# A graph-network kernel whose two planes of edge sums are merged before their product

## The chip, the cores and the metric

One Trainium2 chip, one of its cores. The metric is the device time of one execution in microseconds; lower is better. Five engines work side by side from lists of their own and meet at semaphores: TensorE (PE in the profile; its weight loads are PEld), VectorE (DVE), ScalarE (ACT), GpSimd (POOL) and SyncE (SP, which only issues DMAs here). SBUF is the memory on the chip, with 128 partitions; PSUM holds TensorE's results.

## The reference, cut to what matters

There are 12,500 nodes with 128 features and 200,000 edges, sorted by their target `dst`. Each edge has 64 features for the first layer and 128 for the second.

```python
h = relu(layernorm(x))
aggregated = segment_sum(edge_attr_64 @ W_edge.T, dst) / clip(degree, 1)
x = x + concat([h @ W_self.T, aggregated @ W_neigh.T]) @ W_final.T + b_final
h = relu(layernorm(x))
agg = segment_sum(edge_attr_128, dst)
x = x + relu(concat([h, agg]) @ W1 + b1) @ W2 + b2
```

`degree` is the number of edges that a node receives. All is fp32.

## The kernel before

**Sums over the edges.** The edges are cut into 128 chunks of 12 or 13 units of 128 edges. For every chunk VectorE compares the targets, counted from the first target of a batch, with 0 to 63 (`one_hots`, L1013), which gives a 128 x 64 one-hot matrix a unit. TensorE multiplies each unit's features with it (`sums`, L631, L633, L649): the 128 features of the second layer and the 64 of the first, summed by node into a window of 64 nodes. The degrees come from a product of ones with the sum of the one-hots (L658), which GpSimd adds up (`hot_sums`, L522). VectorE adds each window from PSUM to its place in SBUF (`adds`, L1043), where the first node of the window is only known at run time.

**Three planes.** The sums lie in `agg`, 128 partitions x 3 planes x columns, a column a node. Plane 0 has the 128 features of the second layer. The first layer's sums are spread over planes 1 and 2 so that TensorE's halves can work at once: in plane 1 the features are in partitions 64 to 127 and the degree in 0 to 63, in plane 2 it is the other way round. A node's true sum is the sum of both planes with the halves of one exchanged. `w_c` has a version of the projected weights for each plane, with a column more that picks the degree.

**Groups and ticks.** A tick is one chunk. 25 groups of 512 nodes (the last of `SEQ` has 256) are worked through the two layers as soon as their sums are complete: group q of `SEQ` is taken on tick `TAKE[q]`. Its steps stand at fixed ticks behind that: `neigh` (L694, TensorE, the product of `agg` with `w_c`) at +0, `layer_0` at +1, `stats_2` at +2, `std_2` at +3, `scale_2` at +4, `norm_2` at +5 (L903), its turning by TensorE at +6 (L669) and ScalarE's copy at +7, `hidden` at +8 (L706, L708) and +9 (L918), `output` at +10 (L715), `result` at +11 (L1157) and the store at +12. The part of the layer that needs no edges (`stats_1` to `own_part`, L678, and ScalarE's copies L883 and L890) starts at tick `SELF[q]`, some nine ticks before. On each engine the tick's own work on the chunk (`sums` on TensorE) comes first and these steps behind it, except on VectorE, where the steps come ahead of the tick's `adds`. Nothing is moved at run time: what waits, holds up all that is behind it on its engine.

**What binds ticks to each other.** `sums` use three banks of PSUM in turn, so they wait for the adds of three ticks before. One-hots are made three ticks ahead, edges are loaded into five slots (L394), so that a load waits for the sums five ticks before. `neigh` waits for all adds of the ticks before its own and, in some groups, for a `fold` (L1112, L1114). The columns of a finished group are cleared by GpSimd for another (`CLEARS`). Two groups, 8 and 9 (q = 22 and 23), have two sets of columns (`BOTH`) and twice the products.

Of the kernel before, what the change touches and what calls it, by code (L numbers as in the profile page):

```python
# [14 lines left out]
P = 128  # L15
# [60 lines left out]
def build_gnn(nc, x, dst, edge_attr_128, edge_attr_64, W_self, W_neigh, W_edge, W_final, b_final,  # L76
# [73 lines left out]
    for q, g in enumerate(SEQ):  # L150
        for at, other in ((FIRST_W, g + 4 if g and g in LOWER else 0), (UPPER_AT, g - 4 if g in UPPER else 0)):
            if other in (LOWER if at == FIRST_W else UPPER) and other:
                a = at + (g - 1) % 4 * GW
                CLEARS.append((TAKE[q] + 9, a, a + GW))
# [7 lines left out]
    def bounds(t):  # L162
# [4 lines left out]
        if SIDE[t] == "bottom":  # L167
            lo = min(g for g in free if g) if 1 not in free else 0
            hi = lo
            while hi + 1 in LOWER and hi + 1 in free and (hi < 4 or TAKE[TURN[hi - 3]] + 11 <= t):  # L170
                hi += 1
# [7 lines left out]
        while lo - 1 in UPPER and lo - 1 in free and (lo - 1 > NG - 5 or TAKE[TURN[lo + 3]] + 11 <= t):  # L179
            lo -= 1  # L180
# [41 lines left out]
    for t in range(TICKS):  # L222
        for q in range(NG):
            if t == TAKE[q] + 6:
                tp_use["n", q] = len(tp_use)
            if t == TAKE[q] + 10:
# [24 lines left out]
    with ExitStack() as ctx:  # L251
# [19 lines left out]
        own = sb("own", [P, GN, D])  # L271
        h2 = sb("h2", [P, GN, D])
# [60 lines left out]
        def ps_tab(q):  # L333
# [14 lines left out]
        s_fold, s_nb, s_deg, s_x1, s_bn2, s_mv2, s_std2, s_rstd2, s_nmr2 = (  # L348
            sem(n) for n in ("s_fold", "s_nb", "s_deg", "s_x1", "s_bn2", "s_mv2", "s_std2", "s_rstd2", "s_nmr2"))
# [93 lines left out]
        def _(pool):  # L443
# [58 lines left out]
            def clear(k, a, b):  # L502
                done = [q for q in range(NG) if TAKE[q] + 9 == k]
# [49 lines left out]
            for t in range(TICKS):  # L553
# [4 lines left out]
                for q in range(NG):  # L558
                    if t == TAKE[q] + 6:
# [12 lines left out]
        def _(pe):  # L572
# [108 lines left out]
            def neigh(q):  # L681
                g = SEQ[q]
                pe.wait_ge(s_added, ADDED[min(CH, TAKE[q])])
                for i, (k, _) in enumerate(FOLDS):
                    if k == q:
                        pe.wait_ge(s_fold, 2 * i + 2)
# [4 lines left out]
                parts = [(a, k) for a in columns_of(g) for k in range(2)]  # L691
# [29 lines left out]
            for t in range(TICKS):  # L721
# [10 lines left out]
                for q in range(NG):  # L732
                    if t == TAKE[q] + 8:
                        hidden(q)
                    if t == TAKE[q] + 10:
# [4 lines left out]
                for q in range(NG):  # L740
                    if t == TAKE[q] + 6:
# [4 lines left out]
                for q in range(NG):  # L746
                    if t == TAKE[q]:
# [62 lines left out]
        def _(act):  # L810
# [80 lines left out]

            def std_2(q):
# [27 lines left out]
            for t in range(TICKS + 1):  # L920
# [3 lines left out]
                for q in range(NG):  # L924
                    if t == TAKE[q] + 12:
                        store(q)
                for q in range(NG):
                    if t == TAKE[q] + 7:
                        turned_2(q)
                    if t == TAKE[q] + 9:  # L930
# [6 lines left out]
                for q in range(NG):  # L937
                    if t == TAKE[q] + 3:
# [387 lines left out]
```

## Time and profile before

| | |
|---|---|
| median of 3 runs | 556.91 us (556.08 to 558.59) |
| profiled execution | 556.97 us |
| its span, first to last instruction | 555.1 us |
| TensorE matmuls busy | 503.9 us, 91% |
| VectorE, GpSimd, ScalarE busy | 390.6, 368.4, 151.5 us |
| mean granted TensorE clock | 0.966 of full speed |
| moved by DMA | 169.53 MB, 305 GB/s on average |

The page has the busy time of each engine, the span in slices, the DMA queues, the chain of work that ended last, and the costliest groups of instructions. "Idle before" is the idle time of an engine in front of an instruction, with the instruction that released it; "issue" means that nothing was found that the engine could have waited for. An fp32 product is two records in the trace. Records of TensorE overlap: their mean is longer than the time from one start to the next.

### The profile page before, as it was taken

How to read it: one execution, taken by the hardware profiler on the slowest of the kernel's cores; microseconds unless marked ns; L12 is line 12 of the kernel's file. 1: busy time of each engine (PE TensorE's matmuls, PEld its weight loads, DVE VectorE, ACT ScalarE, POOL GpSimd, SP SyncE). 2: the span in 40 equal slices, each digit the busy share in tenths (PEclk: the TensorE clock that was granted, in tenths of full speed). 3: DMA queues.
4: the chain of work that ended last, by engine and by line, in shares of the span. 5: the costliest groups of instructions: out<-in, count | busy, mean ns of one | idle time of the engine just before them, and what ended most of it. 6: DMA issues, size and time to landing. Idle time of an engine off the chain costs nothing.

```text
span 555.1 us, 25952 instructions
## 1 busy us (share of the span) xinstructions
PE 503.9 (91%) x10989; PEld 450.1 (81%) x10989; DVE 390.6 (70%) x1230; ACT 151.5 (27%) x353; POOL 368.4 (66%) x524
## 2 busy tenths in 40 slices
PE   5568879899989999999999999998999999999993
PEld 4457768789878898888988898888888888988782
DVE  5434698776896768967798688789669877567322
ACT  0011101332233332342234224333323332313101
POOL 2735947667577776785768777885866765845730
PEclk9767899999999999999999999999999999999996
DMA  8924999999999998999999999999999998959910
GB/s 282 388 58 148 380 354 359 374 339 322 312 347 303 341 349 303 367 301 313 341 323 355 333 331 323 369 320 304 325 320 358 329 322 277 382 221 310 378 41 13
DMA packets 113229, 169.53 MB, mean 305 GB/s; under 512 B 5486, under 2 KB 84310, under 8 KB 113111
## 3 DMA queue, kind: packets, MB, share of 16 engines
q1 hardware_dynamic: 85843, 154.42, 79.7%
q10 hardware_dynamic: 27268, 13.43, 8.3%
q8 instruction: 88, 1.44, 1.1%
q14 instruction: 30, 0.25, 0.1%
HBM read 161.43 MB, written 6.40 MB: 302 GB/s over the span
## 4 chain that ended last, share of the span: by engine, by line
PE 81%; issue 6%; DVE 4%; DVEq 1%; ACT 0%; POOL 0%
PE ps L631 28%; PE ps L649 15%; PE ps L694 9%; PE ps L706 5%; PE ps L633 5%; PE ps L678 5%; PE ps L669 4%; PE ps L715 4%; PE ps L708 4%; DVE agg L1043 2%; PE ps L658 1%; DVE x L1157 1%; DVE onehot L1013 1%; DVE bn L1137 0%; DVEq L1043 0%
## 5 line engine op out<-in xcount | busy, mean ns | idle before, releaser
L631 PEld LDWEIGHTS ps<-onehot,ring 128*64 128x64 f32 x3126 | 198.8, 141 | 30.8 <-issue 22.6
L631 PE MATMUL ps<-onehot,ring 128*64 128x64 f32 x3126 | 217.2, 228 | 6.5 <-issue 4.6
L633 PE MATMUL ps<-onehot,ring 128*64 128x64 f32 x3126 | 217.3, 228 | 4.7 <-issue 4.7
L522 POOL TENSOR_TENSOR hot_part<-onehot 128x384 bf16<-128x384 f32 (+2 forms) x128 | 116.7, 912 | 152.3 <-DVE onehot L1013 150.6
L633 PEld LDWEIGHTS ps<-onehot,ring 128*64 128x64 f32 x3126 | 198.8, 141 | 5.4 <-issue 5.4
L1043 DVE TENSOR_TENSOR agg<-ps,agg 128x128 f32 (+1 forms) x319 | 95.0, 298 | 120.1 <-PE ps L658 95.9
L1013 DVE TENSOR_TENSOR onehot<-iota_win,rel 128x384 f32<-128x384 f32 (+3 forms) x192 | 164.5, 857 | 0.2
L649 PE MATMUL ps<-onehot,ring 128*64 128x64 f32 x3126 | 121.9, 226 | 7.2 <-issue 7.1
L649 PEld LDWEIGHTS ps<-onehot,ring 128*64 128x64 f32 x3126 | 109.2, 141 | 7.4 <-issue 7.2
L694 PEld LDWEIGHTS ps<-w_c,agg 128*128 128x128 f32 x424 | 49.8, 191 | 7.3 <-DVE agg L1043 3.7
L694 PE MATMUL ps<-w_c,agg 128*128 128x129 f32 x424 | 52.3, 276 | 3.3 <-issue 2.3
L522 POOL TENSOR_TENSOR hot_sum<-hot_part 128x128 bf16<-128x128 bf16 x96 | 44.7, 466 | 7.5
L875 ACT ACTIVATE hn<-x,nmr,rstd 128x128 f32<-128x128 f32 x98 | 40.4, 483 | 22.5 <-DVE nmr L1104 22.4
L903 ACT ACTIVATE h<-x,nmr,rstd 128x128 f32<-128x128 f32 x98 | 40.4, 484 | 15.5 <-DVE nmr L1149 15.5
L918 ACT ACTIVATE hid<-ps,b_col 128x512 f32<-128x512 f32 (+1 forms) x25 | 17.0, 679 | 93.2 <-PE ps L708 93.2
L500 POOL TENSOR_TENSOR x<-x,b_bc 128x512 f32<-128x512 f32 (+1 forms) x25 | 35.6, 1424 | 10.2 <-ACT h L903 10.2
L522 POOL TENSOR_TENSOR hot_sum<-hot_sum,hot_part 128x128 bf16<-128x128 bf16 x64 | 34.9, 545 | 5.0
L508 POOL MEMSET agg<- 128x1536 f32 (+2 forms) x26 | 35.5, 1366 | 0.0
L487 POOL TENSOR_TENSOR x<-x,b_bc 128x512 f32<-128x512 f32 (+1 forms) x25 | 34.2, 1369 | 0.0
L883 ACT COPY hT<-ps 128x512 f32<-128x512 f32 (+1 forms) x25 | 14.5, 579 | 70.5 <-PE ps L669 70.5
L890 ACT COPY own<-ps 128x512 f32<-128x512 f32 (+1 forms) x25 | 14.5, 579 | 67.3 <-PE ps L678 64.4
L494 POOL TENSOR_TENSOR x<-x,own 128x512 f32<-128x512 f32 (+1 forms) x25 | 31.9, 1275 | 0.0
(118 smaller groups left out, 568.7 us busy)
## 6 DMA issues: line engine op xcount, KB each, us to landing
ring<-in_edge_attr_dram SPq DMA_DIRECT2D x95, 768.0 KB, 5.5
ring<-in_edge_attr_dram SPq DMA_DIRECT2D x96, 384.0 KB, 7.0
ring<-in_edge_attr_dram SPq DMA_DIRECT2D x32, 832.0 KB, 6.2
ring<-in_edge_attr_dram SPq DMA_DIRECT2D x32, 416.0 KB, 7.7
x<-in_x_dram ACTq DMA_DIRECT2D x23, 256.0 KB, 6.3
out_dram<-x ACTq DMA_DIRECT2D x23, 256.0 KB
x<-in_dst_dram SPq DMA_DIRECT2D x1, 384.0 KB
x<-in_dst_dram SPq DMA_DIRECT2D x1, 208.0 KB, 3.6
```

The lines of the kernel that those rows point to most:

```text
L487: nc.gpsimd.tensor_tensor(rows, rows, b0_bc[:, :].unsqueeze(1).to_broadcast([P, nt, D]), ALU.add).then_inc(s_xb, 1)
L500: nc.gpsimd.tensor_tensor(rows, rows, b2_bc[:, :].unsqueeze(1).to_broadcast([P, nt, D]), ALU.add).then_inc(s_x1b, 1)
L508: nc.gpsimd.memset(agg[:, :, a:b], 0.0).then_inc(s_zero, 1)
L522: nc.gpsimd.tensor_tensor(out, a, b, ALU.add).then_inc(s_hotsum, 1)
L631: nc.tensor.matmul(bank[0:H, o:o + WIN], ring128[0:K, slot, u, 0:H], hots, start=u == 0, stop=r == R - 1, skip_group_check=True)
L633: nc.tensor.matmul(bank[H:P, o:o + WIN], ring128[0:K, slot, u, H:D], hots, start=u == 0, stop=r == R - 1, skip_group_check=True)
L649: nc.tensor.matmul(bank[feats, o:o + WIN], ring64[0:K, slot, u, :], onehot[0:K, hot, u, :], start=False, stop=True, skip_group_check=True)
L694: last = nc.tensor.matmul(ps_nb[:, j // 2, j % 2, :], agg[:, 1 + k, a + j * P:a + (j + 1) * P], w_c[:, k, :], start=i == 0, stop=i == len( ...
L875: last = nc.scalar.activation(hn[:, j, :], x0[:, j0 + j, :], ACT.Relu, bias=nmr1[:, u, j:j + 1], scale=rstd1[:, u, j:j + 1])
L903: last = nc.scalar.activation(h2[:, j, :], x0[:, j0 + j, :], ACT.Relu, bias=nmr2[:, u, j:j + 1], scale=rstd2[:, u, j:j + 1])
L1013: made = nc.vector.tensor_tensor(onehot[:, t % HOTS, a:b, :], iota_win[:, :].unsqueeze(1).to_broadcast([P, b - a, WIN]), rel[:, c // 32, a ...
L1043: nc.vector.tensor_tensor(here, ps[:, t % BANKS, o:o + w * WIN].rearrange("p (a n) -> p a n", a=w), here, ALU.add).then_inc(s_added, 1)
```

## The change

For the 22 groups that have one set of columns (`MERGED`), ScalarE copies the lower half of plane 2 into the upper half of a new tile `swapped` and the upper into the lower (`swap`, at tick `TAKE[q]`, the last of ScalarE's steps on that tick). VectorE adds `swapped` to plane 1 (`merge`, at `TAKE[q] + 1`, in front of that tick's adds). `neigh` then issues one product a tile, of plane 1 with `w_c[:, 0]`, where it issued one of each plane. For this, `neigh` and all steps behind it move two ticks back (`NEIGH = TAKE + 2`), except for the last group; so do the clearings, and the own parts, which are placed from it. The rule that places own parts has one more condition: `own_part` no longer falls on the tick of a `result` (`r + 11`), beside that of an `output` (`r + 10`). Groups 8 and 9 and the last keep both products of each set of columns.

```diff
+    MERGED = [q for q, g in enumerate(SEQ[:-1]) if g not in BOTH]
+    NEIGH = [t + 2 if q < NG - 1 else t for q, t in enumerate(TAKE)]
...
-        t = min(TAKE[q] - 9, SELF[0] - 2 if SELF else CH)
-        while any(t + 4 == r + 6 or t + 6 == r + 10 for r in TAKE):
+        t = min(NEIGH[q] - 9, SELF[0] - 2 if SELF else CH)
+        while any(t + 4 == r + 6 or t + 6 in (r + 10, r + 11) for r in NEIGH):
...
+        swapped = sb("swapped", [P, GW])
...
             def neigh(q):
                 g = SEQ[q]
-                pe.wait_ge(s_added, ADDED[min(CH, TAKE[q])])
-                for i, (k, _) in enumerate(FOLDS):
-                    if k == q:
-                        pe.wait_ge(s_fold, 2 * i + 2)
+                if q in MERGED:
+                    pe.wait_ge(s_merged, MERGED.index(q) + 1)
+                else:
+                    pe.wait_ge(s_added, ADDED[min(CH, TAKE[q])])
+                    for i, (k, _) in enumerate(FOLDS):
+                        if k == q:
+                            pe.wait_ge(s_fold, 2 * i + 2)
...
-                parts = [(a, k) for a in columns_of(g) for k in range(2)]
+                parts = [(a, k) for a in columns_of(g) for k in range(1 if q in MERGED else 2)]
...
+            def swap(m):
+                q = MERGED[m]
+                (a,), w = columns_of(SEQ[q]), tiles_of(SEQ[q]) * P
+                act.wait_ge(s_added, ADDED[min(CH, TAKE[q])])
+                for i, (k, _) in enumerate(FOLDS):
+                    if k == q:
+                        act.wait_ge(s_fold, 2 * i + 2)
+                if m:
+                    act.wait_ge(s_merged, m)
+                nc.scalar.copy(swapped[0:H, 0:w], agg[H:P, 2, a:a + w])
+                nc.scalar.copy(swapped[H:P, 0:w], agg[0:H, 2, a:a + w]).then_inc(s_swap, 1)
...
+                for m, q in enumerate(MERGED):
+                    if t == TAKE[q]:
+                        swap(m)
...
+            def merge(m):
+                q = MERGED[m]
+                (a,), w = columns_of(SEQ[q]), tiles_of(SEQ[q]) * P
+                dve.wait_ge(s_swap, m + 1)
+                nc.vector.tensor_tensor(agg[:, 1, a:a + w], swapped[:, 0:w], agg[:, 1, a:a + w], ALU.add).then_inc(s_merged, 1)
```

Everywhere else `TAKE[q]` becomes `NEIGH[q]` in the ticks of the steps behind `neigh`, on all engines.

TensorE, the end of the tick on which the second group is taken (before): its eight products stand behind the turning of the first group.

```order
L649 MATMUL ps<-onehot,ring 64x64 x13
L654 MATMUL ps<-onehot,ones_h 64x64
L658 MATMUL ps<-hot_sum,ones_h 64x64 x2
L669 MATMUL ps<-ident,h 128x128 x4
L694 MATMUL ps<-w_c,agg 128x129 x8
```

The same with the change, two ticks later in the program:

```order
L654 MATMUL ps<-onehot,ring 64x64 x13
L659 MATMUL ps<-onehot,ones_h 64x64
L663 MATMUL ps<-hot_sum,ones_h 64x64 x2
L674 MATMUL ps<-ident,h 128x128 x4
L702 MATMUL ps<-w_c,agg 128x129 x4
```

Four products are left, and what stands around them is the same, since all steps behind `neigh` have moved along with it.

VectorE before, behind the adds of the tick on which the second group is taken (L1043 an add, L1120 to L1128 `layer_0`, L1102 and L1104 `scale_1`):

```order
L1043 TENSOR_TENSOR agg<-ps,agg 128x3x64
L1013 TENSOR_TENSOR onehot<-iota_win,rel 128x768
L1021 TENSOR_LOAD base x2
L1120 TENSOR_SCALAR deg<-ps 128x4
L1123 RECIPROCAL rdeg<-deg 128x4
L1128 SCALAR_TENSOR_TENSOR x<-ps,rdeg,x 128x128 x4
L1102 RECIPROCAL rstd<-std 128x4
```

The same place with the change (L1066 is the add, L1144 the merge, L1125 `scale_1`):

```order
L1066 TENSOR_TENSOR agg<-ps,agg 128x3x64
L1036 TENSOR_TENSOR onehot<-iota_win,rel 128x768
L1044 TENSOR_LOAD base x2
L1144 TENSOR_TENSOR agg<-swapped,agg 128x512
L1125 RECIPROCAL rstd<-std 128x4
```

The merge stands where `layer_0` stood, and `layer_0` comes two ticks later. On ScalarE, at the same group, the swap comes behind the tick's other steps and in front of `norm_2` (L923) of the group before:

```order
L898 COPY own<-ps 128x512
L883 ACTIVATE hn<-x,nmr,rstd 128x128 x4
L875 ACTIVATE std<-mv,eps 128x4
L909 COPY swapped<-agg 64x512
L910 COPY swapped<-agg 64x512
L923 ACTIVATE h<-x,nmr,rstd 128x128 x4
```

Before, the copy of the own part, the statistics and `norm_2` followed each other there without the two copies.

## Rows read from the trace of the kernel before

**Rows 1.** The page: busy us (share of the span) and instructions of each engine.
```profile
PE 503.9 (91%) x10989; PEld 450.1 (81%) x10989; DVE 390.6 (70%) x1230; ACT 151.5 (27%) x353; POOL 368.4 (66%) x524
```
**Rows 2.** Windows: stretch, its length, busy us (instructions) by engine, PEclk, DMA share, GB/s.
```profile
50.00:110.00 60.00, 50.28 (x1333) 47.64 (x1332) 46.29 (x136) 12.50 (x29) 39.27 (x49) 0.97 0.99 348
110.00:480.00 370.00, 360.76 (x7992) 321.22 (x7990) 289.96 (x979) 122.97 (x288) 268.18 (x336) 1.00 0.98 329
```
**Rows 3.** Waits of PE: who waited for whom, us in total, times, longest.
```profile
PE ps L649 <- issue: 7.1, 9, 1.9
PE ps L633 <- issue: 4.7, 5, 2.1
PE ps L631 <- issue: 4.6, 4, 1.7
...
PE ps L694 <- DVE agg L1043: 1.1, 3, 0.6
PE ps L678 <- DVE x L1157: 1.0, 2, 0.7
```
**Rows 4.** Waits of the other engines and of the load queue for PE.
```profile
DVE agg L1043 <- PE ps L658: 95.9, 73, 7.0
ACT hid L918 <- PE ps L708: 93.2, 25, 8.8
SPq L394 <- PE ps L658: 386.7, 123, 13.3
```
**Rows 5.** The chain that ended last: start us, us, what.
```profile
283.96 1.78 PE ps L694 x16
365.57 1.09 PE ps L715 x8
```
**Rows 6.** Groups by line and shape: busy us, mean ns, idle before and releasers.
```profile
L694 PE MATMUL ps<-w_c,agg 128*128 128x129 f32 x424 | 52.3, 276 | 3.3 <-issue 2.3 <-DVE agg L1043 1.1
L1157 DVE TENSOR_TENSOR x<-ps,x 128x512 f32<-128x512 f32 x24 | 16.3, 680 | 0.6 <-PE ps L715 0.6
L883 ACT COPY hT<-ps 128x512 f32<-128x512 f32 x24 | 14.1, 587 | 68.3 <-PE ps L669 68.3
```
**Rows 7.** Timeline, waits of PE: start us, us, engine, line, idle before.
```profile
156.18 2.02 PE L694 MATMUL ps<-w_c,agg 128*128 128x129 f32 x16 [1.43 <-issue]
295.03 1.13 PE L678 MATMUL ps<-w_a,hT 128*128 128x128 f32 x8 [0.72 <-DVE x L1157]
482.34 0.49 PE L694 MATMUL ps<-w_c,agg 128*128 128x129 f32 x3 [0.84 <-issue]
541.97 1.16 PE L694 MATMUL ps<-w_c,agg 128*128 128x129 f32 x8 [0.62 <-DVE agg L1043]
```
**Rows 8.** Timeline from 265 to 280 us, in order of start.
```profile
268.84 0.29 DVE L1043 TENSOR_TENSOR agg<-ps,agg 128x128 f32 x1 [0.19 <-DVE agg L1043]
269.58 1.65 ACT L903 ACTIVATE h<-x,nmr,rstd 128x128 f32<-128x128 f32 x4 [3.14 <-DVE nmr L1149]
270.77 0.28 DVE L1043 TENSOR_TENSOR agg<-ps,agg 128x128 f32 x1
272.76 1.95 PE L694 MATMUL ps<-w_c,agg 128*128 128x129 f32 x16
274.64 0.27 PE L631 MATMUL ps<-onehot,ring 128*64 128x64 f32 x1
274.98 0.29 DVE L1043 TENSOR_TENSOR agg<-ps,agg 128x128 f32 x1 [0.19 <-DVE agg L1043]
276.92 0.44 PE L669 MATMUL ps<-ident,h 128*128 128x128 f32 x2
279.65 0.23 PE L658 MATMUL ps<-hot_sum,ones_h 128*64 128x64 bf16 x4
```
**Rows 9.** The one-hots' line: duration in ns min/median/max, first and last start.
```profile
L1013 DVE TENSOR_TENSOR onehot<-iota_win,rel x192: 541/794/2076, 9.8 to 532.7; 128x384 f32<-128x384 f32 x115, 128x768 f32<-128x768 f32 x44, 128x832 f32<-128x832 f32 x19, 128x448 f32<-128x448 f32 x14
```
**Rows 10.** The page, DMA queues: packets, MB, share of 16 engines.
```profile
q8 instruction: 88, 1.44, 1.1%
```

More of the change, by code:

```diff
@@ L169, in bounds @@
             hi = lo
-            while hi + 1 in LOWER and hi + 1 in free and (hi < 4 or TAKE[TURN[hi - 3]] + 11 <= t):
+            while hi + 1 in LOWER and hi + 1 in free and (hi < 4 or NEIGH[TURN[hi - 3]] + 11 <= t):
                 hi += 1
@@ L178, in bounds @@
         lo = hi
-        while lo - 1 in UPPER and lo - 1 in free and (lo - 1 > NG - 5 or TAKE[TURN[lo + 3]] + 11 <= t):
+        while lo - 1 in UPPER and lo - 1 in free and (lo - 1 > NG - 5 or NEIGH[TURN[lo + 3]] + 11 <= t):
             lo -= 1
@@ L223, in build_gnn @@
         for q in range(NG):
-            if t == TAKE[q] + 6:
+            if t == NEIGH[q] + 6:
                 tp_use["n", q] = len(tp_use)
-            if t == TAKE[q] + 10:
+            if t == NEIGH[q] + 10:
                 row_use["n", q] = len(row_use)
@@ L347, in build_gnn @@
         s_tp, s_tpc, s_row, s_rowc, s_self = (sem(n) for n in ("s_tp", "s_tpc", "s_row", "s_rowc", "s_self"))
-        s_fold, s_nb, s_deg, s_x1, s_bn2, s_mv2, s_std2, s_rstd2, s_nmr2 = (
-            sem(n) for n in ("s_fold", "s_nb", "s_deg", "s_x1", "s_bn2", "s_mv2", "s_std2", "s_rstd2", "s_nmr2"))
+        s_swap, s_merged, s_fold, s_nb, s_deg, s_x1, s_bn2, s_mv2, s_std2, s_rstd2, s_nmr2 = (
+            sem(n) for n in ("s_swap", "s_merged", "s_fold", "s_nb", "s_deg", "s_x1", "s_bn2", "s_mv2", "s_std2", "s_rstd2", "s_nmr2"))
         s_h2, s_x1b, s_hid, s_hr, s_store = (sem(n) for n in ("s_h2", "s_x1b", "s_hid", "s_hr", "s_store"))
@@ L502, in clear @@
             def clear(k, a, b):
-                done = [q for q in range(NG) if TAKE[q] + 9 == k]
+                done = [q for q in range(NG) if NEIGH[q] + 9 == k]
                 if done:
@@ L732, in _ @@
                 for q in range(NG):
-                    if t == TAKE[q] + 8:
+                    if t == NEIGH[q] + 8:
                         hidden(q)
-                    if t == TAKE[q] + 10:
+                    if t == NEIGH[q] + 10:
                         output(q)
@@ L746, in _ @@
                 for q in range(NG):
-                    if t == TAKE[q]:
+                    if t == NEIGH[q]:
                         neigh(q)
@@ L937, in _ @@
                 for q in range(NG):
-                    if t == TAKE[q] + 3:
+                    if t == NEIGH[q] + 3:
                         std_2(q)
-                    if t == TAKE[q] + 5:
+                    if t == NEIGH[q] + 5:
                         norm_2(q)
@@ L1190, in _ @@
                 for q in range(NG):
-                    if t == TAKE[q] + 1:
-                        layer_0(q)
-                    if t == TAKE[q] + 11:
-                        result(q)
-                    if t == TAKE[q] + 2:
-                        stats_2(q)
-                    if t == TAKE[q] + 4:
-                        scale_2(q)
+                    if t == NEIGH[q] + 1:
+                        layer_0(q)
+                    if t == NEIGH[q] + 11:
+                        result(q)
+                    if t == NEIGH[q] + 2:
+                        stats_2(q)
+                    if t == NEIGH[q] + 4:
+                        scale_2(q)
+                for m, q in enumerate(MERGED):
+                    if t == TAKE[q] + 1:
+                        merge(m)
                 for q in range(NG):
```

12 lines of the change are left out of this document (6 added, 6 removed).

## The prediction

> **What bounds the kernel now.** I read the table of engines first. TensorE (PE) is busy 503.9 us of a span of 555.1 us [rows 1]; the next engine, VectorE (DVE), has 390.6 us. A busy share is only a mean, so the windows came next: from 110 to 480 us PE idles 9.2 of 370 us, while DVE idles 80 [rows 2]. The one stretch where PE has real holes is 50 to 110 us, 9.7 us idle of 60, and there the DMA share is 0.99 at 348 GB/s. The waits say what the holes are [rows 3]: PE waits for DVE in 1.1 and 1.0 us, and most of the rest is "issue", idle time in the middle of the sums (L631, L633, L649) for which the profile shows no releaser. In the other direction everybody waits for PE: the adds 95.9 us, ScalarE (ACT) 93.2 us in one line alone, and the queue that loads the edges 386.7 us in 123 waits [rows 4]. So from tick 4 to the end the time is the sum of PE's own instructions, in order, plus a few holes. What is taken off PE's list comes off the time, as long as nobody becomes later than PE was.
>
> **What the change takes off PE.** Here `neigh` issues two products a tile for the 22 groups that have one set of columns, and one after the change; four tiles a group make 22 x 4 = 88 products less. In the trace each such product is two records, and a group of sixteen stands in the chain with 1.78 us [rows 5], so 0.112 us a record. The mean of one record is 276 ns [rows 6], but records overlap: the count times the mean would be 4.4 us a group and is not what a group costs. A group that keeps 8 records gives back 8 x 0.112 = 0.89 us, and 22 groups 19.7 us. The two groups of both regions (8 and 9) and the last one (0) keep their products. Eight records may cost more than half of sixteen: an eight-record group of another product stands in the chain with 1.09 us [rows 5], that is 0.136 a record with the tail of its last one. At that size the kept half would cost 1.09 and the saving would be 0.70 a group, 15.4 us. I take 19.7, because the chain gives a sixteen-record group up to the next one's start, and keep 15.4 as the lower bound of this term.
>
> **Waits that go.** `neigh` of a tick starts only when the adds of the tick before, and a fold, are through. PE idles 3.3 us in front of these products [rows 6]. The largest is 1.43 us at 156.18, in a group that also waits for a fold [rows 7]. After the change the sums are swapped and merged before, and `neigh` comes two ticks later, so this goes. Two parts of the 3.3 stay: 0.62 of the last group, which has no sums behind it, and 0.84 at 482.34, where three of eight products had been issued, so that no semaphore can have held it [rows 7]. 3.3 - 0.62 - 0.84 = 1.9 us go. `own_part` on the tick of a `result` waits for that result in the row bank of PSUM, 1.0 us in two places [rows 3], 0.72 of it at 295.03 [rows 7]; the new rule keeps own parts off these ticks. Sum of what leaves PE: 19.7 + 1.9 + 1.0 = 22.6 us.
>
> **What is added, and beside what it lies.** ScalarE gets 44 copies of 64x512. The nearest row is the copy of 128x512 out of PSUM, 587 ns [rows 6]; from SBUF four 128-wide activations take 1.65 us together [rows 8]. A swap is thus between 2 x 0.59 = 1.2 and 2 x 1.65 = 3.3 us; I take 1.3, nearer the row with the same operation and width. 22 x 1.3 = 29 us on an engine that is busy 151.5 of 555.1. DVE gets 22 adds of 128x512 with both inputs in SBUF. Below: 0.68 us, the same shape with one input in PSUM [rows 6]. Above: the one-hots have two SBUF inputs and take 541, 794 or 2076 ns (min, median, max) [rows 9], so 2.1. I take 1.0, hence 22 us, and keep 46 as the other end. The longest is nearly four times the shortest, and a wider shape explains only twice (768 elements against 384).
>
> The Trainium skill has a rule that fits such a spread (page "SBUF — State Buffer", section "Who interferes with whom"): a VectorE instruction with two SBUF inputs and a GpSimd instruction that reads SBUF exclude each other for the whole instruction. It speaks against the change, since every merge is of that kind. By it the merges cost DVE up to the upper end, and delay the one-hot sums on GpSimd by the same; the time is unchanged as long as both stay hidden. The Trainium skill (page "VectorE: DVE Perf Modes", section "The TRN2 errata") prices a lone fp32 add of 512 from SBUF at 0.69 us; by it the 22 merges would be 15 us, beside PE as well.
>
> **Why it stays hidden.** A swap on ACT waits for the adds of tick t-1, the merge stands on DVE behind the adds of tick t, and `neigh` closes PE's tick t+2. I follow it at the group whose `neigh` stands at 272.76 [rows 8]. The adds that it needs end at 271.05. A swap could end at 272.4, DVE is through with the adds of the following tick at 275.27, the merge ends at 276.3, and the new place of `neigh` is behind the one-hot sums that start at 279.65: 3.3 us spare. Behind the merge on DVE stand the adds of its tick. A bank is written again three ticks later: the tick whose last add ends at 269.13 frees a bank whose sums begin at 274.64, 5.5 us spare, of which a merge of 1.0 or even 2.1 eats a part. Behind the swap on ACT stands, for nine groups, `norm_2` of the group before in the next tick: here it ends at 271.23 and its turn on PE starts at 276.92, 5.7 us spare against 1.3. Its start needs DVE's scale of the same tick, which comes later than the swap's input, so even less is lost. Moving `neigh` and what hangs on it two ticks back moves each wait with its releaser; the store of group 9 comes two ticks later, still ahead of the last group's. The clearings shift by two ticks and no load of edges waits for them.
>
> **What is given back.** The issue holes are 16.4 us of PE in all [rows 3], and more than half lie in 50 to 110 us, where PE idles 9.7. In that stretch two groups halve their `neigh` and one is pushed out of it, 2.7 us of PE work less; if what limits it is the memory traffic, all of this comes back. Behind it DMA must move the same bytes in less time: 329 GB/s becomes 329 x 1.04 = 342, below the 348 that it did move in the first stretch. Loads are waited for by nobody, but the queue named "instruction" [rows 10] shares these engines, and its 88 packets could open a hole more. Between 0 and 4.5 us (the 2.7 of that stretch, and two more holes of the size of the 0.84 [rows 7]); I take 1.6, about a third, since the holes were there with PE's old list as well.
>
> **Sum.** Profiled execution 556.97 us (span 555.1 and 1.9 around it), 556.97 - 22.6 + 1.6 = 536.0. The median of the runs shown is 556.91, the same within 0.1, so the time is 536.0.
>
> **Rivals.**
> - *The memory is the bound behind PE.* For it: DMA share 0.98 from 110 to 480 us [rows 2]. If 329 GB/s were the ceiling from 110 to 480, nothing is gained there and only the tail's few us and half of the first stretch: about 552. Against: the load queue waits for PE, not PE for it [rows 4], and 348 GB/s was moved with a share only 0.01 higher. 4 in 100; a mild form, half of the gain lost, 546, another 4.
> - *A new wait in the relay.* The swap takes 3.3 us, or ACT reaches it late, so `norm_2` or the merge comes later than its spare 3.3 to 5.7 us in some groups, and PE waits 0.3 to 0.5 us at each of 22: 536 + 9 = 545. Against: ACT idles 73% of the span and each of its lines waits for PE. 7 in 100.
> - *DVE becomes the bound, slower than before.* The place is the merge: it waits for the swap at the head of DVE's queue, then for GpSimd's lock, with adds and one-hots of its tick behind it. From 110 to 480 us DVE is busy 290 of 370 us, 80 idle, with 20 groups: it passes PE's old time when a merge with its wait costs 80 / 20 = 4.0 us, twice the longest one-hot. At 4.5 us it is 370 + 10, so 566 us. 3 in 100.
> - *The removed products were half hidden.* The term is 15.4, the rest as above: 540. 10 in 100.
>
> **Chances.** The forecast (531 to 539) has 72 in 100. Runs of this kernel spread by 0.5% at most, 2.8 us, and that is the line of "same". Faster: 72 + 10 + 7 + 4 and most of 4 (552 is 0.9% below), with something held back for what I don't see, 0.93. Same 0.03, slower 0.04. The range: the floor is all of 22.6 and 3 us of issue holes that fall away by chance, 531; the top takes in the half-hidden products and part of the relay's wait, 542.
>
> **What would show it.** The product group in `neigh` has 248 records, 176 less, and stands in the chain with about 0.9 us a group. PE busy falls by about 19 to 20 us, no wait of PE for ACT or DVE in the middle, no wait at `own_part`. The swap's copies read 0.6 us each, the merge 0.7 to 2.1 and around 1.0. DVE busy rises to about 413, ACT to about 178. Issue holes from 110 to 540 stay below 12 us. I am wrong if PE's idle time rises by more than 5 us with a releaser named on ACT or DVE (the relay), or if the load queue no longer waits for PE (the memory).

## The result, and the profile after

The changed kernel takes 552.86 us (median of 8 runs, 544.94 to 555.5) against 558.17 us (554.09 to 559.17) for the kernel before on the same chip; the ratio is 0.9874 [0.9824, 0.9923]. Medians are of all executions; ratios leave out those over 1.5% above the fastest of the same kernel, which are four of the changed kernel's eight. It is faster, but by 5 to 7 us and not by 21: the time lies outside the range given. The profiled execution took 552.04 us, its span is 550.2 us, 4.9 less than before.

The page after, busy us (share of the span) and instructions of each engine, to be held against [rows 1]:

```profile
PE 486.7 (88%) x10813; PEld 432.4 (79%) x10813; DVE 413.1 (75%) x1252; ACT 178.7 (32%) x397; POOL 380.1 (69%) x524
```

TensorE is busy 17.2 us less, close to the 19 to 20 forecast; VectorE and ScalarE stand at the 413 and 178 that were forecast. So the work left and came as foreseen, and the span should have fallen by 17 or more. It fell by 4.9: TensorE idles 12.3 us more. The windows after, with the columns of [rows 2], say where:

```profile
50.00:110.00 60.00, 49.60 (x1364) 47.25 (x1360) 45.73 (x139) 14.09 (x32) 36.77 (x48) 0.94 0.99 343
110.00:480.00 370.00, 347.68 (x7864) 306.88 (x7863) 314.24 (x1003) 148.35 (x329) 286.16 (x342) 1.00 0.99 336
```

From 50 to 110 us TensorE idles 10.4 us (9.7 before), but from 110 to 480 us 22.3, where it idled 9.2. TensorE's waits after (as [rows 3]; "..." stands for waits at the start and the end that the kernel before has as well) say what the idle time is:

```profile
PE ps L654 <- issue: 19.6, 16, 2.2
...
PE ps L663 <- issue: 3.7, 2, 2.1
...
PE ps L638 <- issue: 3.2, 3, 2.6
PE ps L636 <- issue: 2.7, 6, 0.9
PE ps L674 <- issue: 2.1, 1, 2.1
...
PE ps L683 <- issue: 1.0, 1, 1.0
PE ps L723 <- ACT own L898: 0.7, 2, 0.5
PE ps L723 <- ACT hid L938: 0.6, 1, 0.6
```

L636, L638, L654 and L663 are the sums, L674 the turning, L683 the own part, L723 the output. No wait for the merge or the swap is among them, and those of `neigh` for the adds and of the own part for the result are gone, as forecast. But "issue", where nothing that the profile knows holds the engine, is 19.6 + 3.7 + 3.2 + 2.7 + 2.1 + 1.0 = 32.3 us. Before it was 19.3 (the 16.4 of [rows 3], 2.3 in front of L694 [rows 6] and 0.7 of L678, before rounding). These 13.0 us are the greater part of the missing gain.

The new instructions, by form (VectorE's merge, the first of ScalarE's two copies, TensorE's products):

```profile
L1144 DVE TENSOR_TENSOR agg<-swapped,agg 128x512 f32<-128x512 f32 x22 | 18.4, 837 | 0.0
L909 ACT COPY swapped<-agg 64x512 f32<-64x512 f32 x22 | 13.6, 617 | 19.2 <-DVE agg L1066 14.9 <-issue 4.0
L702 PE MATMUL ps<-w_c,agg 128*128 128x129 f32 x248 | 32.5, 278 | 0.0
```

A swap is 2 x 0.617 = 1.23 us (1.3 forecast), a merge 0.84 (1.0). And a group of eight records stands in the chain of waits with just half of the 1.78 us of [rows 5]:

```profile
115.58 0.89 PE ps L702 x8
```

**Where the holes lie.** They come at a fixed distance in TensorE's list. These are windows of the changed kernel from the middle of one hole of about 0.9 us or more to the middle of a later one (the stretch from 100.53 to 110.99 and all behind 194.87 are left out):

```profile
57.89:70.43 12.54, 9.62 (x254) 9.18 (x254) 10.07 (x32) 1.95 (x5) 9.47 (x13) 0.86 1.05 378
70.43:77.13 6.70, 4.51 (x127) 4.22 (x127) 4.63 (x12) 0.59 (x1) 3.33 (x4) 1.00 1.05 384
77.13:88.23 11.10, 8.98 (x254) 8.59 (x253) 10.14 (x28) 2.02 (x4) 5.96 (x9) 1.00 1.04 374
88.23:100.53 12.30, 10.67 (x253) 10.09 (x254) 8.38 (x32) 2.43 (x6) 7.71 (x10) 0.86 0.98 337
110.99:117.93 6.94, 5.40 (x126) 4.96 (x126) 4.91 (x12) 2.72 (x6) 6.78 (x8) 1.00 1.04 380
117.93:145.85 27.92, 26.23 (x633) 23.56 (x633) 21.32 (x67) 9.97 (x21) 21.13 (x24) 1.00 0.99 335
145.85:194.87 49.02, 46.14 (x1010) 40.52 (x1011) 40.88 (x135) 20.02 (x45) 39.47 (x43) 1.00 0.98 328
```

Add the records of PE and PEld: 508, 254, 507, 507, 252, 1266, 2021. Those are 2, 1, 2, 2, 1, 5 and 8 times about 253. With the instructions that the view does not count (semaphores), the raw records give 256 a block. The kernel has 2 x 10,813 records, 85.5 blocks of 253, and the page counts 87 packets of the queue "instruction" (88 before [rows 10]):

```profile
q8 instruction: 87, 1.43, 1.1%
```

So a packet holds the instructions of one block, 16 KB. At 1.1% of 16 engines over 550 us a packet takes 1.1 us on an engine.

The trace also has the time of every packet. In the changed kernel there are 20 issue waits of 0.5 us or more behind 50 us. All stand at an edge of a block, and all end 1.2 to 1.6 us after a packet of this queue has ended. In all 15 kernels of this document with full loads there are 273 such waits. Of these 267 stand at an edge and end 1.2 to 1.7 us after a packet's end; the other six are one place, the first product of `neigh` near 156 us, which waits for a fold. So a block that starts late starts when its packet has come. Packets begin a median of 2.7 us after the edge before and end 3.8 us after it (60 to 480 us), so with the 1.4 us behind the packet a next block is ready about 5.2 us after an edge. The blocks themselves last 4.5 us and more, 5.7 in the median: a short block meets a packet that is not there yet. One such place after, in the timeline of TensorE (start us, us, engine, line, idle before):

```profile
234.41 0.34 PE L654 MATMUL ps<-onehot,ring 128*64 128x64 f32 x5
236.64 0.74 PE L654 MATMUL ps<-onehot,ring 128*64 128x64 f32 x18 [1.89 <-issue]
```

Five products of a run of 24 are through, their operands have long been there, and nothing comes for 1.9 us.

### The profile page after: what moved, and what is told of

It reads as the page before. It is cut to its first block, busy times and chain, and to the rows that moved or that the text cites. A ratio compares the mean times of both kernels' runs of the same rounds, so it can differ in the third digit from the quotient of the medians.

```text
span 550.2 us, 25690 instructions
## 1 busy us (share of the span) xinstructions
PE 486.7 (88%) x10813; PEld 432.4 (79%) x10813; DVE 413.1 (75%) x1252; ACT 178.7 (32%) x397; POOL 380.1 (69%) x524
## 3 DMA queue, kind: packets, MB, share of 16 engines
q8 instruction: 87, 1.43, 1.1%
## 4 chain that ended last, share of the span: by engine, by line
PE 74%; issue 9%; DVE 5%; POOL 3%; DVEq 1%; ACT 0%; ACTq 0%; POOLq 0%
PE ps L636 27%; PE ps L654 15%; PE ps L638 5%; PE ps L723 5%; PE ps L702 5%; PE ps L714 4%; PE ps L674 4%; PE ps L683 4%; PE ps L716 3%; POOL hot_sum L527 1%; POOL hot_part L527 1%; PE ps L663 1%; DVE agg L1066 1%; DVE onehot L1036 1%; POOL x L499 1%
## 5 line engine op out<-in xcount | busy, mean ns | idle before, releaser
L636 PEld LDWEIGHTS ps<-onehot,ring 128*64 128x64 f32 x3126 | 199.5, 141 | 29.5 <-issue 23.2
L636 PE MATMUL ps<-onehot,ring 128*64 128x64 f32 x3126 | 218.1, 228 | 4.7 <-issue 2.7
L638 PE MATMUL ps<-onehot,ring 128*64 128x64 f32 x3126 | 218.4, 228 | 3.2 <-issue 3.2
L527 POOL TENSOR_TENSOR hot_part<-onehot 128x384 bf16<-128x384 f32 (+2 forms) x128 | 118.6, 926 | 132.7 <-DVE onehot L1036 130.5
L638 PEld LDWEIGHTS ps<-onehot,ring 128*64 128x64 f32 x3126 | 199.5, 141 | 3.5 <-issue 3.4
L1066 DVE TENSOR_TENSOR agg<-ps,agg 128x128 f32 (+1 forms) x319 | 94.6, 297 | 104.0 <-PE ps L663 81.8
L1036 DVE TENSOR_TENSOR onehot<-iota_win,rel 128x384 f32<-128x384 f32 (+3 forms) x192 | 169.9, 885 | 0.1
L654 PE MATMUL ps<-onehot,ring 128*64 128x64 f32 x3126 | 124.1, 226 | 19.8 <-issue 19.6
L654 PEld LDWEIGHTS ps<-onehot,ring 128*64 128x64 f32 x3126 | 110.7, 141 | 22.3 <-issue 22.2
L527 POOL TENSOR_TENSOR hot_sum<-hot_part 128x128 bf16<-128x128 bf16 x96 | 49.2, 512 | 7.5
L505 POOL TENSOR_TENSOR x<-x,b_bc 128x512 f32<-128x512 f32 (+1 forms) x25 | 34.1, 1366 | 13.0 <-ACT h L923 13.0
L923 ACT ACTIVATE h<-x,nmr,rstd 128x128 f32<-128x128 f32 x98 | 40.4, 484 | 7.2 <-DVE nmr L1178 7.1
L527 POOL TENSOR_TENSOR hot_sum<-hot_sum,hot_part 128x128 bf16<-128x128 bf16 x64 | 36.2, 565 | 5.0
L492 POOL TENSOR_TENSOR x<-x,b_bc 128x512 f32<-128x512 f32 (+1 forms) x25 | 36.9, 1475 | 0.0
L663 PE MATMUL ps<-hot_sum,ones_h 128*64 128x64 bf16 x382 | 32.3, 195 | 4.1 <-issue 3.7
L499 POOL TENSOR_TENSOR x<-x,own 128x512 f32<-128x512 f32 (+1 forms) x25 | 33.2, 1329 | 0.0
L702 PEld LDWEIGHTS ps<-w_c,agg 128*128 128x128 f32 x248 | 30.3, 193 | 3.2 <-issue 2.9
```

The lines of the kernel that those rows point to most:

```text
L492: nc.gpsimd.tensor_tensor(rows, rows, b0_bc[:, :].unsqueeze(1).to_broadcast([P, nt, D]), ALU.add).then_inc(s_xb, 1)
L499: nc.gpsimd.tensor_tensor(rows, rows, own[:, 0:nt, :], ALU.add).then_inc(s_self, 1)
L527: nc.gpsimd.tensor_tensor(out, a, b, ALU.add).then_inc(s_hotsum, 1)
L636: nc.tensor.matmul(bank[0:H, o:o + WIN], ring128[0:K, slot, u, 0:H], hots, start=u == 0, stop=r == R - 1, skip_group_check=True)
L638: nc.tensor.matmul(bank[H:P, o:o + WIN], ring128[0:K, slot, u, H:D], hots, start=u == 0, stop=r == R - 1, skip_group_check=True)
L654: nc.tensor.matmul(bank[feats, o:o + WIN], ring64[0:K, slot, u, :], onehot[0:K, hot, u, :], start=False, stop=True, skip_group_check=True)
```

## The experiments

The theory: TensorE waits for its own instructions. They come by DMA, a block of 256 at a time, and beside saturated edge loads a new block takes about as long to come as one runs. Work taken off TensorE makes blocks shorter and turns into such waits. The rivals: the relay (swap and merge) costs the gain; the removed products were worth less; the new rule for own parts costs it.

The "light" kernels show what happens without the traffic, though their results are no longer right. They load edges on 16 of 128 partitions from tick 7 on:

```diff
+                    k = P if t < 7 else 16
-                    sp.dma_start(ring[:, slot, ...], feats[e0:e1, :]...)
+                    sp.dma_start(ring[0:k, slot, ...], feats[e0:e1, :]...[0:k])
```

**Light loads, before and after.**

> The kernel before, but from the eighth tick on each edge load brings only 16 of 128 partitions (the number of DMAs and every instruction of every engine stay, the rest of a slot keeps old edges). Theory A (TensorE stops at the end of a block of 256 of its own instructions until the next block has been fetched, and the fetch waits among the edge loads): the issue holes behind tick 8, some 17 us in the trace of before, shrink to a few, so about 557 - 15 = 542 us. Rival B (the relay of swap and merge delays TensorE through buffers and semaphores): says nothing of this kernel; the holes are no matter of DMA, 555 to 558. Rival C (edge loads themselves are the bound): TensorE never waited for them in the trace, but if they were it, 530 or less.

> The changed kernel with the same lighter loads. Theory A: the holes of the changed kernel, about 33 us behind tick 6, shrink to what is left in the lighter kernel before, so the difference between the two light kernels is what was predicted for the products and waits, 20 to 23 us: about 521 us. Rival B: the difference between the light kernels stays at the 5 to 7 us of the full ones, 535 to 550. Rival C: both light kernels are faster, with no rule for their difference.

e1: 538.22 us, ratio to the kernel before 0.9685 [0.9627, 0.9743]. e2: 530.84, 0.9542 [0.949, 0.9594]. TensorE's waits with light loads in the kernel before (start-up left out):

```profile
PE ps L695 <- DVE agg L1044: 2.9, 4, 1.1
...
PE ps L695 <- issue: 1.5, 1, 1.5
PE ps L679 <- DVE x L1158: 1.0, 3, 0.5
```

and in the changed kernel:

```profile
PE ps L724 <- ACT own L899: 12.0, 4, 3.9
...
PE ps L637 <- issue: 0.3, 1, 0.3
```

The issue waits fall from 19.3 to 1.5 and from 32.3 to 0.3 us: edge traffic makes them. What changes is when a packet begins, 0.5 and 0.4 us after the edge (median) instead of 2.8 and 2.7; the packet itself takes 1.0 to 1.1 us at either load. TensorE's busy time also falls, by 6.9 us (497.0) and 6.6 (480.1), with the same instructions, and no run says why. But the changed kernel gains only 7.4 us here too, not the 20 to 23 expected, since a new wait of 12.0 us shows, that of the output for ScalarE's copy of the own part. That was not in my theory. A load of x of the same 256 KB in both shows what the traffic does to a transfer (KB each, median us from issue to landing), before:

```profile
x<-in_x_dram ACTq DMA_DIRECT2D x23, 256.0 KB, 6.3
```

and with light loads:

```profile
x<-in_x_dram ACTq DMA_DIRECT2D x23, 256.0 KB, 3.0
```

**Half of the change at a time.** One product a tile without relay or moved steps (the second plane's sums are left out), and the relay with both products kept:

```diff
-                parts = [(a, k) for a in columns_of(g) for k in range(2)]
+                parts = [(a, k) for a in columns_of(g) for k in range(1 if g not in BOTH and q < NG - 1 else 2)]
```
```diff
-                parts = [(a, k) for a in columns_of(g) for k in range(1 if q in MERGED else 2)]
+                parts = [(a, k) for a in columns_of(g) for k in range(2)]
```

> The kernel before with one product a tile in the 22 groups (only plane 1 is multiplied, so half of each neighbour sum is left out), no swap, no merge, no shift by two ticks, own parts where they were. Theory A: the products alone are worth as little as the whole change, because the faster list runs into the fetches: 549 to 553 us. Rival B: without the relay the products are worth their 19.7 us, 537 us.

> The changed kernel with swap, merge, the shift and the new rule for own parts, but with both products a tile again (plane 2 is counted twice, so the neighbour part is too large). Theory A: the relay costs TensorE nothing and its list is the old one, with 2.9 us of waits gone: 553 to 557 us. Rival B: the relay costs what is missing, some 13 us, 567 to 570.

e3: 546.70 us, 0.9814 [0.9733, 0.9895]; TensorE busy 486.4, issue waits 28.5. e4: 567.62, 1.0212 [1.0154, 1.027]; busy 505.3, issue waits 30.2. Even the bare removal brings 10 us, not 20, with no relay to blame: busy falls by 17.5 and issue waits rise by 9. e4 costs 11 us though TensorE's work is unchanged. That is the rival's number, 567 to 570; the theory's 553 to 557 was missed, and e3 lies 2 us below its 549. But TensorE waits for no swap or merge in it; its longest waits are issue waits again, and packets begin 2.6 us after an edge, as in the kernel before (2.8). So the relay does not slow the packets. What it changes for TensorE is the order of the list, and that this order costs the 11 us is argued here; the next runs bear on it.

**The list shifted.** n small products of 64x1 on tick 0 move all that follows by 2n instructions against the edges of the blocks:

```diff
                 if t == 0:
+                    for _ in range(n):
+                        nc.tensor.matmul(ps[0:H, 2, 0:1], ones_h[:, :], ones_h[:, 0:1], start=True, stop=True)
                     bases()
```

> The kernel before with 32 small products (one column, 64 records with their weight loads) behind the sums of the first tick, where TensorE waits for VectorE anyway. They move every later instruction of TensorE's list by 64 against the edges of its blocks of 256. Theory A2 (the list of before stood luckily against those edges: its short blocks met quick fetches, and any other position costs what the change lost): holes at the edges rise from 20.5 to 30 or more, 562 to 572 us. Rival B2 (it is the relay's traffic on ScalarE and VectorE that makes fetches or TensorE slower): the position is no matter, 555 to 559 us.

> The same with 64 small products, the list 128 further. A2: 562 to 572 us. B2: 555 to 559 us.

> The kernel before with 96 small products of 64x1 on the first tick: TensorE's list is shifted by 192 instructions. Theory (at the unshifted place the short blocks met quick packets by chance, any other place is dearer): 563 to 570 us, as at shifts of 64 and 128. Rival (the shifts differ at random around one mean): 552 to 560 comes out as often.

> The changed kernel with the 32 small products. A2: its 36 us of holes are an ordinary position, so a shift gives anything from 540 to 557 us, and the spread between positions is several us. B2: 551 to 554 us.

> The changed kernel with 64 small products. A2: 540 to 557 us, and different from the shift by 64. B2: 551 to 554 us.

> The changed kernel with 96 small products of 64x1 on the first tick, its list shifted by 192 instructions, the partner of the kernel before at the same shift (562.0 us, 6 above its unshifted self). Theory (the changed kernel has no lucky place to lose): 551 to 559 us, so at equal shift the change is worth 3 to 11 us. Rival (a shift by 192 costs each kernel its 6 us): 557 to 561.

| shift | before, us (ratio) | issue waits | after, us (ratio) | issue waits |
|---|---|---|---|---|
| 0 | 555.5 to 558.2 | 19.3 | 552.86 (0.9874) | 32.3 |
| 64 | 567.20 (1.0223 [1.0137, 1.0309]) | 21.2 | 557.17 (1.0021 [0.9988, 1.0054]) | 34.5 |
| 128 | 565.62 (1.0191 [1.0135, 1.0247]) | 24.2 | 555.22 (0.9993 [0.9961, 1.0025]) | 35.0 |
| 192 | 562.02 (1.0105 [1.0047, 1.0163]) | 23.1 | 549.02 (0.9856 [0.9804, 0.9907]) | 22.3 |

All ratios are to the unshifted kernel before on the same chip; the issue waits are those of the profiled execution. In every shifted kernel the long waits stand at the same multiples of 256 records, the added ones counted, so the edges did move against the program. The control has the same 32 products (shift 64), but in front of the sums of tick 124:

> The control for the two kernels with extra small products on the first tick: the same 32 products of 64x1, but in front of the sums of tick 124, so that only the last few per cent of TensorE's list is shifted. Theory (where the edges of the blocks of 256 instructions fall makes the difference): the products cost what they cost TensorE, 1 to 5 us, and the time is 557 to 561 us against 556 before, with 'issue' waits as before (19 us in all). Rival (the 32 products themselves cost the 10 us, wherever they stand): 566 us again.

It took 556.52 us, 0.9995 [0.9957, 1.0033]. So the products cost nothing that can be measured; where they stand, and so what they shift, is what costs 11 us. The kernel before stood at the best of its four places; the fourth, at 562.0, is just under the 563 expected. (The changed kernel at shift 64 is as narrowly above its 557.) At equal shifts of 64, 128 and 192 the change is worth 10.0, 10.4 and 13.0 us (the last pair ran on two chips), unshifted 5.3 by the medians, 7 by the ratio. The changed kernel at shift 192 has the lowest median of all full kernels, 549.0, under the 551 expected, but its interval overlaps that of the unshifted one: no version here is shown to beat it.

The waits do not account for all of a shift. The 30 us of holes and more that were expected of the kernel before did not come, it has 21 to 24. At 64 the span of before grows by 8.5 us: TensorE's idle time by 3.1 and its busy time by 5.4, of which the 32 small records are some 1.3 (64 of them have 2.6 at shift 128). The control has as many and its busy time is 503.6. What makes the rest of the busy time stays open, and with it why one place is cheaper than another.

**Fewer loads in flight.**

```diff
                 if t >= SLOTS:
                     sp.wait_ge(s_mm, t - SLOTS + 1)
+                    sp.wait_ge(s_load[(t - 2) % SLOTS], LOADED[t - 2])
```

> The changed kernel, where the load of a tick's edges is also held until the load of two ticks before has landed, so that at most two or three chunks are in flight. Theory (the instruction packets are slow because they stand behind queued edge loads): with fewer of them queued the packets are quicker, the issue waits of 32 us shrink by some 5 to 15 us and the time is 540 to 549 us. Rival A (what slows the packets is the rate at which edges move, not the length of the queue: the rate is the same): within 0.5% of the changed kernel, 550 to 556. Rival B: SyncE starts loads late and TensorE waits for edges, above 558.

> The kernel before with the same hold on the edge loads (two ticks before must have landed). Theory (quicker packets): issue waits of 19 us fall by 5 to 10 us, 546 to 551 us. Rival A (rate, not queue, slows the packets): 554 to 559. Rival B (loads come late): above 560.

g2: 552.65 us, 0.9864 [0.9773, 0.9955], with issue waits of 26.2 us (32.3 without the hold) in a profiled execution of 548.8 us; g4: 559.07, 1.0014 [0.997, 1.0059], with issue waits of 16.8 us (19.3 without), and TensorE now waits 5.7 us for edges. No gain is shown, though g2's interval is wide. The runs cannot tell whether the length of the queue slows the packets, because the hold hardly shortened it. The load queue now waits for landings rather than for TensorE, but each load lands as late after its issue as before, at the same rate. The commonest load without the hold and with it (KB each, median us to landing):

```profile
ring<-in_edge_attr_dram SPq DMA_DIRECT2D x95, 768.0 KB, 5.4
```
```profile
ring<-in_edge_attr_dram SPq DMA_DIRECT2D x95, 768.0 KB, 5.5
```

The packets are no quicker either: they begin 2.9 us after an edge (2.7 without the hold).

**Half loads** (64 of 128 partitions).

> The changed kernel with edges loaded on 64 of 128 partitions from tick 7 on (half of the edge features are left out): a DMA share between the full 0.99 and the light 0.25. Theory (what delays the packets with instructions is that the DMA engines have no free time): at a share near 0.5 the issue waits of TensorE almost vanish, under 6 us of 32, 529 to 535 us. Rival (each further load slows the packets in proportion): about half of them stay, 14 to 18 us, 538 to 545.

545.41 us, 0.9825 [0.9769, 0.988]; issue waits 20.2, and 7.9 for the copy of the own part. Neither number was met, the rival's is nearer. From 110 to 480 us the bytes are nearly halved, the busy share of the DMA engines is not:

```profile
110.00:480.00 370.00, 355.59 (x8012) 314.45 (x8013) 314.71 (x1010) 150.78 (x334) 292.12 (x346) 0.99 0.85 185
```

and x's 256 KB still take 5.5 us. Packets begin 1.9 us after an edge. From 50 to 110 us the bytes are nearly halved as well, but the DMA engines are as busy as with full loads:

```profile
50.00:110.00 60.00, 46.94 (x1321) 44.53 (x1317) 47.70 (x142) 13.69 (x30) 39.22 (x50) 0.97 0.99 196
```

There the issue waits are 13.1 us of the 60, no fewer than the 10.4 of the changed kernel at 343 GB/s. From 110 to 480 us, at nearly the same GB/s but a share of 0.85, they are 6.3 us instead of 20.9. So the waits follow the busy share and not GB/s. A share near 0.5, which the theory spoke of, was not reached.

**Product, relay and rule apart, at light loads.** Half products on the kernel before (the second plane left out, no relay); and the changed kernel with the old rule for own parts:

```diff
-        while any(t + 4 == r + 6 or t + 6 in (r + 10, r + 11) for r in NEIGH):
+        while any(t + 4 == r + 6 or t + 6 == r + 10 for r in NEIGH):
```

> The kernel before with one product a tile in the 22 groups (no exchange, no merge, and so the second plane's sums are left out of the first layer; nothing is moved) and with edges loaded on only 16 of 128 partitions from tick 7 on (most edge features are left out). Against the kernel before with the same light loads (538.2 us). Theory (88 products are worth 17 to 20 us of TensorE's time, and with full loads a part of it is lost to waits for instructions): 518 to 522 us. Rival (the products are worth about 10 us themselves, as the full-load run of half of them showed): 527 to 530.

> The changed kernel with the old rule for the own parts (they may fall on the tick of a result again), edges loaded on only 16 of 128 partitions from tick 7 on (most edge features are left out). With the new rule and the same light loads it took 530.8 us and its outputs waited 12.0 us for the copy of the own part. Theory (the new spacing of own parts crowds GpSimd's add, and this cost is real wherever instructions come in time): the 12 us go, 519 to 523 us. Rival (the exchange and the merge make these waits): they stay, 529 to 532.

g3: 523.64 us, 0.9415 [0.9363, 0.9467]. h1: 523.50, 0.9415 [0.9373, 0.9457]. So where instructions come in time, the products are worth 538.2 - 523.6 = 14.6 us, less than the 17 to 20 expected, the whole relay costs nothing (523.5 against 523.6), and the new rule costs 530.8 - 523.5 = 7.3. In g3 TensorE is busy 477.6 us, 19.4 less than in e1, just the 19.7 of the forecast, but 5 us come back as waits that were covered:

```profile
PE ps L679 <- DVE x L1158: 3.3, 4, 1.3
PE ps L695 <- DVE agg L1044: 3.2, 4, 1.3
PE ps L695 <- issue: 2.5, 2, 2.0
...
PE ps L716 <- ACT own L891: 1.2, 1, 1.2
```

In h1 the wait of the output is nearly gone, and the own part waits for the result instead:

```profile
PE ps L684 <- DVE x L1187: 5.3, 3, 3.0
...
PE ps L724 <- ACT own L899: 2.0, 1, 2.0
```

The rule's wait is a chain over three engines. With it, ScalarE's copy waits longer for GpSimd, which has not yet added the own part of the group before (e2, then h1):

```profile
ACT own L899 <- POOL x L500: 27.2, 5, 7.6
```
```profile
ACT own L899 <- POOL x L500: 13.6, 4, 4.0
```

**The rule at full loads**, undone in the changed kernel (the diff above) and alone in the kernel before:

```diff
-        while any(t + 4 == r + 6 or t + 6 == r + 10 for r in TAKE):
+        while any(t + 4 == r + 6 or t + 6 in (r + 10, r + 11) for r in TAKE):
```

> The changed kernel with the old rule for the own parts, full loads. Theory (the issue holes set the time): 548 to 560 us, the sum of issue waits again 25 to 36 us, no wait of TensorE for ScalarE's copy, and own_part waits for a result again, about 1 us. Rival (the new rule was what cost the forecast gain): 538 to 543.

> The kernel before with the new rule for own parts alone (no own part on the tick of a result); nothing is left out. The prediction priced it at -1.0 us, with the waits of own_part for the result gone. At light loads the same rule cost the changed kernel 7 us, by outputs that wait for the copy of the own part. Theory (at full loads TensorE is late enough that those waits are covered, and the moved list costs a few us at the issue waits): 555 to 566 us, at most 2 us of waits for the copy. Rival (the rule saves its 1.0 us): 554 to 556. Other rival (its waits appear here too): above 560 with 5 us or more of waits of TensorE for ScalarE's copy.

h2: 554.15 us, 0.995 [0.991, 0.999], with 32.8 us of issue waits. i2: 560.31, 1.0052 [1.002, 1.0085]; own_part's wait for the result is gone, as forecast, TensorE does not wait for the copy, and issue waits are 22.2. So at full loads the rule's own cost is covered, and undoing it frees nothing: TensorE comes late enough to hide it. Alone, the rule costs the kernel before 0.5% rather than saving 1.0 us, with 2.8 us more of busy time and 2.9 more of issue waits; that this comes of the moved list is argued.

One difference stays. h2 has the relay and half the products, e3 half the products alone, and h2 takes 7.5 us more by the medians (0.995 against 0.9814). In their profiles TensorE is busy 486.4 us in both, TensorE waits for no swap or merge, and of the 4.0 us between the spans issue waits make 4.4. So the relay may have a price at full loads, but it comes as late instructions. Packets begin 2.8 us after an edge in both, which speaks for the place of the list, but no run separates the two: e3 was not run at other shifts.

## Why the prediction was wrong

- **What bounds the kernel: right in part.** TensorE's list sets the time, but not by its work alone. The 19.3 us of issue waits were on the page; I read them as a few accidents. They are the visible end of a second bound, the delivery of instructions. (The prediction also counted only the 16.4 of [rows 3] as all of them.)
- **Products, 19.7 us: nearly right as work.** Eight records stand in the chain with 0.89 us, as worked out. Busy time fell by 17.2 us at full and 19.4 at light loads (half products alone). As time it is 14.6 at light loads, since 5 us return as covered waits (g3). The lower bound, 15.4, was nearer, though for another reason than its tail.
- **Waits that go, 1.9 and 1.0: right as rows.** Both are absent after, and so are the 0.62 and 0.84 that were to stay: L702 has no idle time in front of it. The 1.43 at 156.18 was no edge of a block, the 0.84 was one. The own-part rule, though, opens a 12.0 us wait as soon as instructions come in time (e2), which the prediction did not price: it moved own parts together and I asked only what TensorE waits for, not who needs the row bank and GpSimd's add behind it.
- **Swap, merge and "why it stays hidden": right.** 1.23 and 0.84 us against 1.3 and 1.0, no wait of TensorE for them at either load, and 0 us for the relay at light loads. The merges take 0.67 to 1.28 us, so the rule cited from the Trainium skill (page "SBUF — State Buffer", section "Who interferes with whom") did not bring them to the one-hots' 2.1; the lone price of 0.69 us was close to the quickest.
- **"What is given back": the step that failed.** I took 1.6 us, at most 4.5, as the 2.7 us of work missing from 50 to 110 us, and two holes more of 0.84. Measured, it is 13.0 us of issue waits, all of it in 110 to 480 us (7.8 before, 20.9 after), where I had counted on fewer than 12 in all up to 540. I had named the queue "instruction" and its 88 packets, but did not divide: 15,982 records in 370 us [rows 2] are 253 in 5.9 us, 88 packets over 555 us one in 6.3. The next block is ready only some 5.2 us after an edge. With so little between them a short block is a hole, and taking out slow products (0.11 us a record, where the 127 of the window from 70.43, mostly sums, take 4.5 us, 0.04 each) pulls more quick ones into the same block.
- **The rivals.** None was it. The memory rival came nearest (552 forecast at 4 in 100, 552.9 measured), and e1 and e2 show busy DMA behind the loss, but not by its mechanism: no edge was waited for. A wait for the relay and a binding VectorE are refuted, by the waits at full loads and by h1 against g3 at light ones.

The sum by measured terms: -17.2 busy, -2.1 waits gone, +13.0 issue, +0.7 for the copy and a remainder of +0.7 is the -4.9 of the span. The profiled execution is 16.0 us above the forecast: 11.4 are issue waits (13.0 less the 1.6 taken), 2.5 the products (19.7 less 17.2), 0.8 waits that went (2.9 less 2.1), 1.4 the last two terms. (The 1.43 us at 156.18 stand under "issue" here, as in the profile. Counted with the waits that went, these are 3.5 us, more than forecast, and what was given back is 14.4.) That the kernel before stood at the best of four places is luck and a part of these: at the other shifts the same change is worth 10 to 13 us.

Shown: the waits come at block edges, end when a packet has come, and vanish with the edge traffic, which makes packets begin late and not take longer; and the time depends on what a shift of the list moves. Only argued: that packets begin late since they stand behind edge packets at each DMA engine. Open: why the unshifted list of before is cut well, what makes TensorE's busy time rise by some us in shifted lists and fall with light loads, and the 7.5 us between h2 and e3.

## What to carry to other kernels

Where an engine executes a long unrolled list, count its records from one "issue" wait to the next. If the counts are multiples of one number, divide its records by the packets of the queue "instruction" and hold the time of one block against the time that the next one takes to come; if they are near each other, "issue" is a bound and not noise, and work removed can come back as such waits. Judge an edit of such a list at several shifts of the list before its ratio is believed, since the place alone moved the time by 8 to 11 us here, as much as the edit. And try an edit once with light loads: that shows what it would be worth, and which of its waits are only covered.

## What the runs showed of the hardware

- TensorE's instructions come in packets of 16 KB for 256 instructions. Where the DMA engines are busy 0.96 to 1.01 from 110 to 480 us, its issue waits are 17 to 35 us of some 555 (shifts and holds included), at 0.25 to 0.26 they are 0.3 to 2.5. With half loads they are 13.1 us in a stretch of 60 at a share of 0.99 and 6.3 in one of 370 at 0.85, with 196 and 185 GB/s.
- A packet of instructions takes 1.0 to 1.1 us (1.3 with half loads). It begins 2.6 to 3.0 us after the edge before at full loads, 1.9 at half, 0.4 to 0.5 at light ones (medians), and TensorE goes on 1.2 to 1.7 us after its end.
- Halving the bytes by using half of the partitions took the busy share of the DMA engines only from 0.99 to 0.85 (336 to 185 GB/s) in one stretch and not at all in another (0.99 at 343 and at 196 GB/s).
- ScalarE copied 64x512 fp32 from SBUF to the other half of the partitions in 0.617 us, about as long as 128x512 from PSUM (0.587). VectorE's add of two SBUF inputs of 128x512 took 0.67 to 1.28 us (median 0.71).
